# Two FFN tile pieces ahead of each autocorrelation stage on ScalarE and GpSimd, and four stages at other tiles, in a four-stage transformer sandwich

## What is computed

```python
f = jnp.fft.rfft(xh, axis=-1)
corr = jnp.fft.irfft(f * jnp.conj(f), n=L, axis=-1)
weights, delay = jax.lax.top_k(corr, top_k)
tmp_corr = jax.nn.softmax(weights, axis=-1)
...
delays_agg = jnp.sum(pattern * tmp_corr[..., None], axis=-2)
```

## Time and profile before

| | |
|---|---|
| median of 3 runs | 835.62 us (835.37 to 836.76) |
| the profiled execution, its own time | 838.06 us |
| its span | 836.3 us |
| TensorE matmuls busy | 732.5 us, 88% |
| VectorE busy | 620.6 us, 74% |
| ScalarE busy | 352.1 us, 42% |
| GpSimd busy | 283.6 us, 34% |
| TensorE's mean granted clock | 0.958 of full |

### The profile page before, as it was taken

How to read it: one execution, slowest core, us unless ns; L and a number is a source line. 1 busy time by engine, 2 the same in 40 slices (tenths; PEclk the granted TensorE clock), 3 DMA queues, 4 the chain that set the end, 5 groups by cost and what they waited for, 6 DMA issues and landing times.

```text
span 836.3 us, 15378 instructions
## 1 busy us (share of the span) xinstructions
PE 732.5 (88%) x5402; PEld 434.2 (52%) x5402; DVE 620.6 (74%) x1306; ACT 352.1 (42%) x683; POOL 283.6 (34%) x334
## 2 busy tenths in 40 slices
PE   0997789999999999888969988899989999899994
PEld 0563233443434433323447766567767767667772
DVE  6725897778677686972799999986797896787703
ACT  0222126656566565764024435445443523432321
POOL 4025331121212212322115563557435334243341
PEclk9999869999999999979989999899999999899998
DMA  8699976844655344363613496712582111120200
GB/s 206 185 213 294 269 191 140 175 89 111 146 114 121 85 80 122 103 173 85 189 38 62 93 197 149 161 26 103 94 164 27 26 39 26 26 51 13 39 26 25
DMA packets 140924, 93.65 MB, mean 112 GB/s; under 512 B 112024, under 2 KB 119064, under 8 KB 140552
## 3 DMA queue, kind: packets, MB, share of 16 engines
q1 hardware_dynamic: 134416, 76.09, 40.2%
q10 hardware_dynamic: 6208, 11.28, 4.3%
q0 software_dynamic: 240, 5.51, 3.2%
HBM read 48.73 MB, written 29.04 MB: 93 GB/s over the span
## 4 chain that ended last, share of the span: by engine, by line
PE 52%; DVE 23%; DMA 7%; ACT 6%; issue 5%; POOL 4%; SPq 3%; ACTq 0%; DVEq 0%; POOLq 0%
PE ps L1258 16%; PE ps L1565 9%; PE ps L1280 8%; PE ps L1529 6%; DVE mx L1414 6%; PE ps L1542 5%; PE ps L1236 5%; DMA qp_d<-arena 2%; ACT arena L1502 2%; DVE mx L1416 1%; DMA arena<-in_L_attn_Wkv_dram 1%; POOL arena L1397 1%; PE ps L1532 1%; DVE rstd L253 1%; PE ps L1791 1%
## 5 line engine op out<-in xcount | busy, mean ns | idle before, releaser
L1258 PE MATMUL ps<-arena 128*128 128x256 f16 (+1 forms) x1952 | 234.3, 276 | 6.7 <-DMA arena<-arena 6.6
L1258 PEld LDWEIGHTS ps<-arena 128*128 128x128 f16 (+1 forms) x1952 | 194.8, 100 | 49.2 <-issue 8.2
L1502 ACT ACTIVATE arena<-ps 128x1024 f32<-128x1024 f32 (+7 forms) x256 | 159.7, 651 | 104.5 <-PE ps L1542 100.4
L1414 DVE TENSOR_REDUCE mx<-ps 128x1 f32<-128x512 f32 (+1 forms) x256 | 156.2, 652 | 33.0 <-PE ps L1532 18.7
L1087 POOL TENSOR_TENSOR arena<-arena 128x256 f32<-128x256 f32 (+1 forms) x100 | 83.2, 832 | 233.0 <-ACT arena L978 230.7
L1529 PE MATMUL ps<-arena 96*128 (+4 forms) x384 | 129.4, 352 | 23.5 <-DVE mx L1414 7.2
L1280 PE MATMUL ps<-arena 128*128 128x512 f16 (+2 forms) x488 | 122.8, 382 | 18.2 <-POOL arena L1093 18.1
L1542 PE MATMUL ps<-arena 99*128 (+4 forms) x384 | 122.5, 336 | 9.3 <-ACT arena L1502 7.7
L1397 POOL TENSOR_SCALAR_AFFINE_SELECT arena<-arena 128x512 f32<-128x512 f32 x64 | 41.8, 654 | 207.8 <-ACT arena L1502 207.8
L1529 PEld LDWEIGHTS ps<-arena 96*128 96x128 bf16 (+1 forms) x384 | 38.5, 100 | 109.3 <-issue 48.7
L1565 PE MATMUL ps<-arena 128*32 128x256 f32 (+1 forms) x1280 | 83.5, 369 | 5.0 <-POOL arena L1397 4.5
(11 more groups left out here) (160 smaller groups left out, 842.4 us busy)
## 6 DMA issues: line engine op xcount, KB each, us to landing
arena<-qp_d SPq DMA_DIRECT2D x48, 128.0 KB, 4.9
lora_d<-arena ACTq DMA_DIRECT2D x20, 256.0 KB, 6.0
arena<-lora_d SPq DMA_DIRECT2D x10, 512.0 KB, 5.6
w1n_d<-arena SPq DMA_DIRECT2D x10, 512.0 KB, 3.7
arena<-rec_d SPq DMA_DIRECT2D x32, 128.0 KB, 2.8
qp_d<-arena SPq DMA_DIRECT2D x12, 256.0 KB, 8.4
w1dn_d<-arena SPq DMA_DIRECT2D x4, 704.0 KB, 4.5
arena<-in_L_ffn_down_w_dram SPq DMA_DIRECT2D x4, 688.0 KB, 4.1
```

The lines of the kernel that those rows point to most:

```text
L1258: last = nc.tensor.matmul(ps[0:h, b, CH * o:CH * (o + 1)], w(t[0])[:, kt, ht * P:ht * P + h], xt[:, c, t[1], kt, :], start=(kt, t) == (0, ...
L1414: nc.vector.reduce_max(to[:, h, t:t + 1], s_bank(g, u)[:, 0:w], mybir.AxisListType.X).then_inc(s_taken, 1)
L1502: nc.scalar.activation(probs[:, kt % 2, h, kt * P:T], st_bank(h).rearrange("p b n -> p (b n)")[:, kt * P:T], ACT.Exp, scale=HD ** -0.5).th ...
```

## The change

Two things. On ScalarE and GpSimd, at a tile n at which a stage stands (`staged`), the piece of tile n - 1 (`act_high`, `pool_low`) is now issued ahead of the stage, where it stood behind the eviction or product of tile n. GpSimd's list of staged tiles holds its own two tables and all five of ScalarE's; ScalarE's list holds its own five. And five numbers change, in five tables: chunk 0's correlation from tile 29 to 30 and its lag terms from 29 to 32; chunk 3's row spectrum, its eviction and its low pieces from 76 to 75.

```diff
-        ROWS_AT = (27, 46, 64, 76)
-        CORR_AT = (29, 48, 65, 76)
+        ROWS_AT = (27, 46, 64, 75)
+        CORR_AT = (30, 48, 65, 76)
...
-        TAKE_AT = (28, 46, 64, 76)
-        LAGS_AT = (29, 54, 66, 77)
+        TAKE_AT = (28, 46, 64, 75)
+        LAGS_AT = (32, 54, 66, 77)
...
-        PLOW_AT = (28, 46, 64, 76)
+        PLOW_AT = (28, 46, 64, 75)
...
         def act_rest(act):
             act.wait_ge(scales0_ready, 1)
             for n in range(TILES):
+                staged = n in TAKE_AT + LAGS_AT + WTAKE_AT + PROD_AT + BTAKE_AT
+                if staged:
+                    act_high(act, n - 1)
                 for c in range(NCH):
...
                 act_tile(act, n)
-                if n > 0:
+                if n > 0 and not staged:
                     act_high(act, n - 1)
             act_high(act, TILES - 1)
...
         def pool_rest(pool):
             for n in range(TILES):
+                staged = n in PLOW_AT + QLOW_AT + TAKE_AT + LAGS_AT + WTAKE_AT + PROD_AT + BTAKE_AT
+                if staged:
+                    pool_low(pool, n - 1)
                 for c in range(NCH):
...
                 pool_product(pool, n)
-                if n > 0:
+                if n > 0 and not staged:
                     pool_low(pool, n - 1)
             pool_low(pool, TILES - 1)
```

## The result

| | before | changed |
|---|---|---|
| median, runs of this comparison | 836.43 us (833.86 to 838.26) | 833.03 us (829.51 to 837.92) |
| ratio | | 0.9958, 95% interval 0.9939 to 0.9977 |
| the profiled execution, its own time | 838.06 us | 831.26 us |
| its span | 836.3 us | 829.5 us |
| TensorE matmuls busy | 732.5 us | 729.8 us, 88% |

The change is faster by 3.4 us, 0.42% (0.23 to 0.61%), where 8.2 had been forecast. One execution of the changed kernel was disturbed (over 2400 us) and is left out of the range. The median, 833.03, lies above the forecast range of 823.0 to 832.0.

A forecast was written before the change was run, and what follows sets the result against it. The prediction took TensorE's stops at autocorrelation stages, and the slow clock after long ones, as the bound, capped where other engines' results come late. The lead ended at 8.2 us: median 835.62 becomes 827.4, range 823.0 to 832.0.

The forecast's parts named there:

- the price of the wait at tiles 45 to 48: Chunk 1's spectrum 3.1 us later, so its correlation waits for back-transform copies: 1.3 to 1.4 lost, TensorE's lead +5.0.
- the 2.0 that VectorE was to gain in chunk 0: VectorE's 2.05 us idle before the products of the spectra goes, leaving it 2.0 ahead until chunk 1's peaks.
- the low clock behind the stops at tiles 56 and 69: Tile 56 was forecast at full speed after 1.7 us idle; no slow clock was charged at tile 69.
- ledger: Running count of how much earlier TensorE is than in the old trace, capped where another engine's result is late.
- Chunk 0: Correlation at tile 30, lag terms at 32: +7.6 us at tile 35, capped to +6.4 at the weight spectra.
- (600.9 and 602.7) are 2.0 earlier: Chunk 1's last peaks on VectorE come 2.0 us earlier, so the lag terms at tile 54 end at 603.3.
- the 7.7: TensorE's forecast lead in us at chunk 1's weight spectra, capped from +8.6 by VectorE and the DMA.
- Chunk 2: Lag terms start 0.85 us later, lead falls to +6.85; product pieces later at tile 73, lead +6.35.
- rival B: Part is eaten: low clock at tile 69 (2.0) and 2.55 at tile 80, 829.8 or 831.8 us; chance 0.22.
- Chunk 3: Row spectrum at tile 75: no stop before correlation, 3.8 us before weight spectra, 2.2 low clock; lead ends at +8.2.
- Rival C: Slower: 0.85 us added to each stage's own chain, 12.7 over 15 staged tiles of chunks 1 to 3, 839.8; chance 0.06.

The follow-up runs named there:

- order_only: The changed kernel with the five table numbers of before, so only the pieces ahead of the stages; ratio 1.0024 to the kernel before.
- no_66_77: The changed kernel with tiles 66 and 77, the lag terms of chunks 2 and 3, out of both staged lists; 828.58 us, 0.9907 to the kernel before.
- changed_again: The changed kernel itself, unaltered, run and profiled once more; 832.0 us, ratio 0.9954 to the kernel before.
- spectra_later: The changed kernel with the weight spectra of chunks 2 and 3, and ScalarE's copies of them, one tile later (70, 81); ratio 0.9905 to the kernel before.
- pick1: The changed kernel, only tiles 28, 32, 54, 62, 66, 77 staged; weight spectra of chunks 2 and 3 at 70, 81, chunk 3's back transform at 84; 0.9881 to before.

## Why the prediction was wrong

The sign was right, the size over twice too large. Two steps failed: the price of the wait at tiles 45 to 48, and the 2.0 that VectorE was to gain in chunk 0. A third term, the low clock behind the stops at tiles 56 and 69, was put at nothing. The prediction's ledger against the ground of the two traces of the changed kernel:

| place | forecast | measured |
|---|---|---|
| weight spectra, chunk 0 | 6.4 | 5.2, 5.7 |
| correlation, chunk 1 | 5.0 | 3.0, 1.5 |
| weight spectra, chunk 1 | 7.7 | 4.2, 2.8 |
| back transform, chunk 2 | 6.35 | 1.6, 0.2 |
| end | 8.2 | 4.8, 3.8 |

- **Chunk 0** was right in kind: stops of 0.65, 1.7 and 0.5 were forecast, 0.59, 0.55, 1.81 and 1.09 came, and the stop for the DMA at the weight spectra stood there, 1.02 (in the second trace it did not, and the ground was 5.7). The table switch took what the earlier trace rows gave. ScalarE of the changed kernel:

```profile
526.17 1.28 ACT L980 ACT_TABLE_LOAD   x1
527.47 0.47 ACT L980 ACTIVATE arena<-ps,sc 128x256 f32<-128x256 f32 x1
```

  1.30 from its start to Silu. The Trainium skill ("ScalarE: Activation LUTs", What ACT_TABLE_LOAD costs) has 2.66 by its sum; this trace, too, does not agree.
- **The first step that failed** is the price in "1.3 to 1.4 lost, **+5.0**", at tiles 45 to 48. The mechanism stood in the prediction, down to the order of the pieces, but its price was read at the wrong waiter. It followed the copies of the back transform to the correlation. The back transform itself waits for its banks until the spectrum of chunk 1 is squared, and stopped 2.65 and 2.92, the second time with the low clock behind it (4.39 for 2.78). From the row spectrum of chunk 1 to its correlation TensorE lost 2.8 and 4.7 of ground (5.85 to 3.03, 6.13 to 1.45).
- **The second step that failed** is "VectorE gains too ... so VectorE is 2.0 ahead until the peaks of chunk 1", and with it "(600.9 and 602.7) are 2.0 earlier". A wait of 2.05 was taken for 2.05 of gain. L846 came 0.93 earlier in one trace and 0.6 later in the other (52.47), and by the first L793 it was level or 1.0 behind (59.73). The last peak of chunk 1 was 1.6 and 0.6 later. Nothing shortens the piece between: behind L793 comes a wait of 5.7 to 5.8 for a transfer that SyncE issues only behind the store of VectorE's own result (`down_store`, then `down_load`), then the same row of work, 27.7 to 29.2 from the second L793 to the last peak.
- **What each of them is of the missing ground.** In the first trace 3.5 is missing at the weight spectra of chunk 1. Of it, 2.0 was missing at tile 48 already, 1.4 of that for the wait at tile 47 beyond its forecast; 1.5 is the low clock at tile 56 (4.31 for 2.78), which the prediction had at full speed; VectorE's late peaks held ScalarE up by 0.24 only. In the second trace 4.9 is missing, 3.5 of it at tile 48, and ScalarE's pause stopped TensorE 1.95 between; the peaks held up nothing. The VectorE step is still what keeps the 7.7 out of reach: with the wait at tile 47 taken away ScalarE waits 2.45 and 1.37 for the peaks, and the ground at the weight spectra of chunk 1 is 5.1 and 5.5. In the times, taking the wait at tile 47 away gave nothing (831.86 against 832.0), so how the loss divides is read from two pairs of profiles and not shown by an experiment. No run moved VectorE's own work.
- **Chunk 2** "costs there", by the forecast, 0.85, and no clock. Measured at the back transform: 2.6 lost since the weight spectra of chunk 1, in both traces, forecast 1.35. The low clock behind a stop there (1.7) had been left to rival B; the stop of 2.25 in the earlier trace rows had cost none.
- **Chunk 3** gave 3.2 and 3.6 from there to the end, forecast 1.85. The row spectrum at tile 75 did what was worked out: no stop before the correlation, one of 3.1 and 2.5 on the DMA before the weight spectra, where 3.8 was forecast, and a low clock behind it that cost 1.7 and 1.6, where 2.2 was. So the errors behind chunk 1 nearly cancel, which is luck.
- **Rival C** ("The piece put ahead lengthens each stage's own chain by 0.85") was given 0.06, on the ground that most places have the slack. As a mechanism it is in the measured time: order_only is slower by 0.24%, and no_66_77 gets 3.4 us back from two places, by its profile 0.6 as a shorter chain (0.3 of ground lost from the row spectrum to the weight spectra of chunk 2, against 0.9 in changed_again) and most of the rest as low clock that does not come.

## What to carry to other kernels

An idle time in front of an instruction is an upper bound of what its engine can gain there; follow that engine to its next result that someone waits for before entering it in a sum, and look for a round trip (store, load) on the way. Put small work ahead of a stage only where the stage blocks that work for long; where a stage is itself waited for, its chain gets longer by the piece, and two short stops can merge into one that costs the clock. Where a stage waits for a transfer, another tile ahead of it and a shorter chain gave the same here (spectra_later 0.9905, no_66_77 0.9907). The tile moves the wait to the next stage if that one's inputs come later too: spectra_later stopped 1.61 and 2.42 at the back transforms; pick1, with fewer pieces put ahead and one back transform moved, 0.60 and nothing.
